# Waiting for landings: a wait added to one loop of gathers, and one moved a group back in a loop of scatters

## The reference

```python
h = jnp.maximum(_layernorm(x, axis=-1), 0.0)
x = x + layer(h, edge_index, ...)
```

## Time and profile before

| | us |
|---|---|
| median of three runs | 6813.45 |
| lowest, highest | 6809.85, 6828.54 |
| the profiled execution, its own time | 6818.45 |
| its span in the profile | 6816.7 |
| GpSimd busy, of the span | 4312.2 |
| first and last gather of the counts, start | 64.7, 700.9 |
| first and last final scatter, start | 6237.3, 6790.7 |

### The profile page before, as it was taken

How to read it: one execution, slowest core, us unless ns; L and a number is a source line. 1 busy time by engine, 2 the same in 40 slices (tenths; PEclk the granted TensorE clock), 3 DMA queues, 4 the chain that set the end, 5 groups by cost and what they waited for, 6 DMA issues and landing times. The chain is left out here.

```text
span 6816.7 us, 44787 instructions
## 1 busy us (share of the span) xinstructions
PE 2985.1 (44%) x13056; PEld 2276.1 (33%) x13056; DVE 3659.4 (54%) x8917; ACT 1166.9 (17%) x1912; POOL 4312.2 (63%) x3949
## 2 busy tenths in 40 slices
PE   5789999934443444376645442111111004453000
PEld 2477655523332333266534332111111003332000
DVE  8755799965554665743356667433322096775000
ACT  0266545512221233111111110000000000000000
POOL 5777455557662666366756665888888705666665
PEclk9899999956665555566566665555555556776555
DMA  2122222211112222122222222222222243111001
GB/s 41 23 69 62 76 67 66 67 37 16 18 18 62 53 58 64 40 87 88 83 69 57 57 57 73 40 40 35 40 27 21 11 153 99 49 52 24 6 6 43
DMA packets 283354, 350.11 MB, mean 51 GB/s; under 512 B 133518, under 2 KB 204432, under 8 KB 281970
## 3 DMA queue, kind: packets, MB, share of 16 engines
q1 hardware_dynamic: 112158, 295.24, 13.0%
q0 software_dynamic: 169376, 41.40, 7.6%
q10 hardware_dynamic: 1576, 10.60, 0.6%
HBM read 231.06 MB, written 122.29 MB: 52 GB/s over the span
## 5 line engine op out<-in xcount | busy, mean ns | idle before, releaser
L2338 POOL DMA_INDIRECT acc<-l_rows,l_uniq x392 | 623.0, 1589 | 120.9 <-issue 108.1
L2559 POOL DMA_INDIRECT l_ring<-t_last,idx x392 | 395.4, 1009 | 401.0 <-ACTq L2554 207.4
L1473 POOL DMA_INDIRECT g_ring<-t_gat,idx x392 | 409.2, 1044 | 317.2 <-POOLq L120 109.4
L2379 PE MATMUL ps_l<-l_msg,l_alike 128*128 128x16 f32 x784 | 176.2, 376 | 976.3 <-DVE l_msg L2442 976.3
L1803 POOL DMA_INDIRECT r_ring<-t_rel,idx x392 | 417.2, 1064 | 271.6 <-issue 104.6
L795 POOL DMA_INDIRECT t_sort<-pay,c_pos x392 | 385.9, 984 | 309.0 <-DVE c_pos L861 208.6
L507 POOL DMA_INDIRECT pay<-in_x,gidx x392 | 463.5, 1182 | 173.8 <-issue 108.7
L2114 POOL DMA_INDIRECT r_ring<-t_rel,idx x392 | 389.9, 995 | 263.6 <-DMA r_ring<-t_rel,idx 116.7
L887 PE MATMUL ps_c<-plane,c_hit 128*128 128x400 f32 x1568 | 542.6, 499 | 1.1 <-ACT c_hit L813 1.1
L2324 POOL DMA_INDIRECT l_ring<-t_mix,idx x392 | 423.3, 1080 | 172.4 <-issue 116.4
L2379 PEld LDWEIGHTS ps_l<-l_msg,l_alike 128*128 128x128 f32 x784 | 170.9, 330 | 981.6 <-DVE l_msg L2442 981.6
(11 more groups left out here) (529 smaller groups left out, 8074.1 us busy)
## 6 DMA issues: line engine op xcount, KB each, us to landing
c_rows_d<-row_dst SPq DMA_DIRECT2D x98, 256.0 KB, 3.3
l_keys<-row_at SPq DMA_DIRECT2D x49, 512.0 KB
l_typs<-row_typ SPq DMA_DIRECT2D x49, 512.0 KB
g_hs<-t_gat SPq DMA_DIRECT2D x30, 660.0 KB
acc<-r_zero SPq DMA_DIRECT2D x60, 320.0 KB
t_rel<-r_row SPq DMA_DIRECT2D x30, 640.0 KB, 3.5
r_hs<-t_rel SPq DMA_DIRECT2D x30, 640.0 KB
d_gain<-acc SPq DMA_DIRECT2D x30, 640.0 KB, 5.9
```

What stands on the lines that cost most here:

```text
L1473: pool.indirect_dma_start(ring[:, s % (NR * QN), :], None, t_gat2, bass.IndirectOffsetOnAxis(idx2[:, s:s + 1], 0)).then_inc(gat_in[s // BA ...
L2338: pool.indirect_dma_start(acc[r], bass.IndirectOffsetOnAxis(uniq[:, s:s + 1], 0), rows[:, (s // ES) % RR, s % ES, :], None, compute_op=ALU.add
L2559: pool.indirect_dma_start(ring[:, s, :], None, t_last, bass.IndirectOffsetOnAxis(idx2[:, s:s + 1], 0)).then_inc(gat_in[s // BATCH], 16)
```

## The change

`spaced` is a new function. It makes the engine wait at every slot, and for the group two in front of the slot's own (the scatters 9 to 16 back, at the least). The final scatters use it in place of `paced`. The gathers of the counts, which had no such wait, get `paced`, behind the holds that they have.

```diff
@@ -60,6 +60,14 @@
     n = s // BATCH - 1
     if s % BATCH == 0 and n >= first // BATCH:
+        engine.wait_ge(landing[n], 16 * BATCH)
+
+
+def spaced(engine, landing, s):
+
+
+    n = s // BATCH - 2
+    if n >= 0:
         engine.wait_ge(landing[n], 16 * BATCH)
@@ -504,6 +512,7 @@
                             hold(pool, hist_ok, s // 2 - 1)
                         elif joins > 0 and turn_no not in (2, 5):
                             hold(pool, act_ok, joins)
+                        paced(pool, gat_in, s)
                         pool.indirect_dma_start(pay[:, s, 8:PAY], None, x,
                                                 bass.IndirectOffsetOnAxis(gidx[:, s:s + 1], 0)
                                                 ).then_inc(gat_in[s // BATCH], 16)
@@ -2565,7 +2574,7 @@
                             hold(pool, final_ok, s // QN + 1)
                         if s == T:
                             hold(pool, final_ok, NE + 1)
-                        paced(pool, sent, s)
+                        spaced(pool, sent, s)
                         pool.indirect_dma_start(fin, bass.IndirectOffsetOnAxis(home_i[:, s:s + 1], 0),
                                                 X[:, s, :], None).then_inc(sent[s // BATCH], 16)
```

## The result

The changed kernel takes 6806.26 us in the median of 14 runs (6795.38 to 6812.76), the kernel before 6817.12 in 14 runs beside it (6808.86 to 6828.63). The ratio is 0.9981, 95% interval 0.9972 to 0.9989: faster by 0.2%, some 11 us, where 49 were forecast. 6806 lies above the range of 6752 to 6788, and within the 0.3% that the prediction calls no change.

The account below looks back on a forecast made before the run. The prediction took the pitch of POOL's final scatters to set the end. Scatters -58.4 and counts +9.5 gave -48.9 us from 6813.45, so 6764.5 us, range 6752 to 6788.

Parts of the forecast that it names:

- The tail: Final scatters: 49 landing waits go, 58.8 us less; 0.4 back for ten scatters with two waits; -58.4 us.
- scatters that back up: Final scatters: without group waits POOL stands for a queue place, 1.41 us per scatter, +177, about 6944 us; chance 0.04.
- another wait in its place: Final scatters: `final_ok` or the barrier replaces the landing wait, so no gain; 6823 or 6813 us; chance 0.02.
- 34 x 1.5: Counts behind the histogram: 34 group heads wait 1.8 us where 0.30 stood; 51 us added.
- late landings under a bulk store: Counts: paced gathers cost as at line 2114 while SyncE stores in bulk; +20 to +36, 6775 to 6791; chance 0.14.
- The relief of "6 us": Counts behind the histogram: VectorE stretches fewer gathers while POOL stands waiting; 6 us saved.
- The room of 17.0 us: End of the counts: the last gather may slip from 700.9 to 717.9 at no cost, 9.7 us before the next phase.
- The histogram: Counts up to the 113th gather: 20 us of added waits against a hold worth 18.5; 2 us remain.
- The absorbed holds: Counts behind the histogram: POOL falls behind and finds its VectorE holds met; 31.1 us absorbed.
- The second wait at 0.48: Counts: a hold ahead of a head's landing wait costs 0.48 us; 6 in the histogram, 10.6 at 22 later heads.
- the upper bound of the text: Counts: 2.65 us per head wait instead of 1.8, giving 53.4 us later, or +36.
- Its lower bound: Counts: 1.70 us per head wait, nothing for the second wait; 10.5 us, inside the room, so 0 us.

Follow-up runs that it names:

- load_once_split: Changed kernel with SyncE's pair of bulk transfers gone: loads of `x` left out from the third on, the 800 KB store cut into five; 6824.06 us, on a slower chip.
- last_group: Changed kernel, but at the end of the counts POOL waits for the last group alone, not for all 49; 6815.11 us.
- heads_no_hold: Changed kernel, but count gathers at the head of a group carry no hold on the compute, the landing wait alone; 6788.13 us.
- all_two_back: Kernel before, with final scatters and every loop of plain gathers except the counts waiting for the group two back; 6394.41 us (ratio 0.9386), on a slower chip 8015.16.
- final_only: Kernel before with only the final scatters changed, the counts left without group waits; 6760.62 us, ratio 0.9914.

## Why the prediction was wrong, point by point

- **The tail: right.** -58.0 measured, -58.4 forecast; the mechanism as put, with 0 instead of 0.4 for the ten double waits and 0.8 of longer issues that the forecast had not. Neither rival of the tail (scatters that back up, another wait in its place) showed: no scatter takes more than 1.46 us, and the median stays 958 ns.
- **The counts: the step that failed is the size of the wait at a head, "34 x 1.5".** It was taken from line 1133, near the lower row and the median landing. The gaps sum to 95.6 instead of 71.8: **+24**. The other 27 heads came out as priced (57.0 against 57.2); the excess is that of seven, six of them beside SyncE's pair, and load_once_split, which has no pair, gives 73.9. The "late landings under a bulk store" stood in the text as a rival at 0.14, with line 2114's 2.65 us as its price. Its mechanism is what happened. The mean of 95.6 / 34 = 2.81 us, second waits included, lies even below that rival's 2.65 + 0.31. What took the time past its +36 are the two terms below.
- **The relief of "6 us" failed.** POOL stands 60 us more, but its gathers are not stretched less: they take 309.4 us behind the histogram, before 307.1. That is +2.3 instead of -6: **+8**. Why is open.
- **The room of 17.0 us failed.** It came from 9.7 us between the last DMA and the next phase after the scatters. Here it is 13.0: **+3.3**. last_group shows that the 48 waits at the end aren't it; what it is stays open.
- The histogram: 3.2 instead of 2, **+1**. The absorbed holds: the forecast of 31.1 was right. The gaps behind the histogram's last hold had 31.3 us above 0.3 each before, and those that are no heads have 0.2 left after.
- The second wait at 0.48 was right (heads_no_hold: 0.44 to 0.49).

9.5 + 24 + 8 + 3.3 + 1 = 45.8, and 46.1 were measured. Each missed term had the same sign, and the upper bound of the text had moved only one of them upward. Its lower bound left out the 2 us of the histogram (it is 12.5, not 10.5), which changes nothing, as both lie inside the room.

## What to carry to other kernels

A wait for the group two back costs nothing (0.31 against 0.30 us) as long as the landings (7.6 us at most here) are shorter than its eight pitches. A wait for what was just issued costs what is left of the landing when the issue ends, 1.4 us above the plain gap in an ordinary case here, and that landing is no constant: price it by what else moves at the moment that the last DMA of the group is issued, not by the median. For a loop that "has room", take the room from the same phase's own end, and let every term of the sum run to its bad side at once before giving a range. Try a change of the pacing on several chips before keeping it: all_two_back beat the kernel before by 418 us on one chip and lost to it by 1123 on another. final_only beat the kernel before by 61 us on its chip, and its median lies 46 us below that of the changed kernel, which was not run beside it; it was not tried on the slower kind.

## What was not expected of the hardware

- A gather of 8 KB that lands in 2.4 us in the median lands in 7.2 when SyncE's 800 and 625 KB start at the same moment (7.5 at most), though the DMA engines together are at most 86% busy in any 2 us of the stretch looked at.
- A second wait ahead of a DMA costs 0.44 to 0.49 us behind a wait that was not met, and nothing behind one that was (slot 40: 0.31).
- The last GpSimd DMA of the counts stands 13.0 us ahead of the next phase, against 9.7 after the accumulating scatters; cause open.
- Two of the four chips of the experiments ran the kernel before 1.1% slower (6892 and 6897 against 6812 and 6821), and on one of them all_two_back took 25% longer than on a chip of the other kind (8015 against 6394). Why is open.
